# Cross attention and a recurrent block: two attention steps per unit on TensorE, side work reordered

## The reference

```python
q = q.reshape(b, l, KVH, GROUPS, HD).transpose(0, 2, 3, 1, 4)
scores = jnp.einsum('bkgld,bksd->bkgls', q, k) * scale + encoder_attention_mask[:, :, None, :, :]
attn = jax.nn.softmax(scores, axis=-1)
out = jnp.einsum('bkgls,bksd->bkgld', attn, v)
x = _ln(out @ Wo + bo + hidden_state) * gamma + beta            # first layer
xxx = jnp.einsum('blfd,fde->blfe', jnp.tanh((xa + sx * maa_x) @ maa_w1)..., maa_w2)
w = jnp.exp(-jnp.exp(time_decay + jnp.tanh(xw @ td_w1) @ td_w2))
def step(s, rkvw):                                              # 256 tokens in turn
    a = k_t[..., :, None] * v_t[..., None, :]
    out = jnp.einsum('bhi,bhij->bhj', r_t, u * a + s)
    s = a + w_t[..., :, None] * s
    return (s, out)
x1 = x + group_norm(out) * silu(g) @ Wo.T
return x1 + sigmoid(xr2 @ Wfr.T) * (square(relu(xk2 @ Wfk.T)) @ Wfv.T)
```

## Time and profile before

| | us |
|---|---|
| median of the runs | 1290.37 |
| the profiled execution, its own time | 1290.32 |
| its span, first to last instruction | 1288.5 |
| PE busy | 1080.8 (84%) |
| ACT busy | 875.5 (68%) |
| DVE busy | 661.7 (51%) |
| POOL busy | 366.3 (28%) |
| mean granted TensorE clock | 0.933 |

### The profile page before, as it was taken

How to read it: one execution, slowest core, us unless ns; L and a number is a source line. 1 busy time by engine, 2 the same in 40 slices (tenths; PEclk the granted TensorE clock), 3 DMA queues, 4 the chain that set the end, 5 groups by cost and what they waited for, 6 DMA issues and landing times.

```text
span 1288.5 us, 18192 instructions
## 1 busy us (share of the span) xinstructions
PE 1080.8 (84%) x7100; PEld 372.0 (29%) x7100; DVE 661.7 (51%) x1113; ACT 875.5 (68%) x953; POOL 366.3 (28%) x381
## 2 busy tenths in 40 slices
PE   3065999899899989999899989998999989997554
PEld 1011122232233323332233223331433223323312
DVE  5322141647463755556464746476465445454473
ACT  1045989777877777777877787777778877794001
POOL 6103023135111532144203522153213200340270
PEclk9567999999999999999999999999999989998666
DMA  5533405170514323261406141342306020500130
GB/s 186 136 92 114 94 1 141 45 128 2 131 34 101 58 91 66 70 97 46 94 26 131 28 125 40 83 76 92 65 11 97 3 40 11 75 1 1 19 55 10
DMA packets 65565, 87.47 MB, mean 68 GB/s; under 512 B 8208, under 2 KB 48192, under 8 KB 65472
## 3 DMA queue, kind: packets, MB, share of 16 engines
q1 hardware_dynamic: 63536, 82.91, 29.5%
q0 software_dynamic: 1936, 3.32, 0.9%
HBM read 50.74 MB, written 18.62 MB: 54 GB/s over the span
## 4 chain that ended last, share of the span: by engine, by line
PE 58%; ACT 14%; DVE 13%; issue 8%; POOL 3%; DMA 2%; SPq 2%; DVEq 0%; ACTq 0%; POOLq 0%
PE psum L702 56%; ACT probs L640 10%; DVE row_max L1124 3%; PE psum L800 1%; DVE o_raw L1171 1%; PE psum L794 1%; DVE k_c L1220 1%; POOL vs L532 1%; SPq L317 1%; DVE k_stack L1435 1%; DMA ctx_t<-in_mask 1%; ACT L640 1%; POOL vs L544 1%; DMA vs<-v_c 1%; DVE xa L1211 1%
## 5 line engine op out<-in xcount | busy, mean ns | idle before, releaser
L640 ACT ACTIVATE probs<-psum 128x1024 f32<-128x1024 f32 (+1 forms) x832 | 807.1, 1023 | 282.6 <-PE psum L702 279.0
L702 PE MATMUL psum<-probs,v_aug 128*9 128x512 f32 (+1 forms) x3328 | 446.8, 609 | 20.8 <-DVE o_raw L1171 20.6
L702 PE MATMUL psum<-q_stack,k_stack 64*128 64x512 bf16 (+1 forms) x1664 | 323.3, 396 | 49.3 <-ACT probs L640 39.9
L702 PEld LDWEIGHTS psum<-q_stack,k_stack 64*128 64x128 bf16 (+1 forms) x1664 | 83.2, 95 | 520.5 <-ACT probs L640 342.2
L527 POOL TENSOR_TENSOR xm<-tmp,xa 128x512 f32<-128x512 f32 x40 | 42.9, 1091 | 235.8 <-DVE tmp L1231 235.8
L1124 DVE TENSOR_REDUCE row_max<-psum 128x8 f32<-128x1024 f32 x64 | 78.0, 1218 | 53.9 <-PE psum L702 53.6
L544 POOL TENSOR_TENSOR vs<-r_c,vs 128x512 f32<-128x512 f32 x64 | 77.7, 1215 | 91.4 <-DVE vs L1242 91.4
L514 POOL TENSOR_TENSOR rstd<-moments,eps 128x2 f32<-128x2 f32 x24 | 4.9, 206 | 311.5 <-DVE moments L1197 311.5
L1242 DVE TENSOR_TENSOR_SCAN vs<-w_c,vs 128x514 f32<-128x514 f32 x64 | 88.9, 1389 | 3.5 <-POOL vs L532 1.1
L532 POOL TENSOR_TENSOR vs<-k_c,vs 128x512 f32<-128x512 f32 x64 | 83.4, 1308 | 23.6 <-DVE r_c L1373 15.0
L702 PEld LDWEIGHTS psum<-probs,v_aug 128*9 128x9 f32 (+1 forms) x3328 | 50.2, 88 | 126.5 <-issue 106.8
(11 more groups left out here) (175 smaller groups left out, 1134.6 us busy)
## 6 DMA issues: line engine op xcount, KB each, us to landing
vs<-v_c SPq DMA_DIRECT2D x64, 257.0 KB, 7.7
ctx_t<-in_mask SPq DMA_DIRECT2D x8, 1601.0 KB, 7.1
k_stacked<-k_parts SPq DMA_DIRECT2D x48, 200.1 KB
k_stack<-k_stacked SPq DMA_DIRECT2D x32, 300.2 KB, 6.5
ctx_t<-in_ctx_t SPq DMA_DIRECT2D x24, 400.0 KB, 5.0
q_stacked<-q_parts SPq DMA_DIRECT2D x96, 64.0 KB, 2.0
q_stack<-q_stacked SPq DMA_DIRECT2D x32, 192.0 KB, 6.7
ctx_t<-in_ctx_t SPq DMA_DIRECT2D x8, 401.0 KB, 3.3
```

The source lines that it names most:

```text
L640: nc.scalar.activation(probs[turn_step % NP][t][0:w, :, :], ps[t][0:w, :, :], ACT.Exp).then_inc(exped.sem, 1)
L702: return nc.tensor.matmul(dst, lhsT, rhs, start=start, stop=stop)
```

## The change

TensorE now walks the steps in pairs. A unit is: both score tiles of the even step, both weighings of the two steps before, both score tiles of the odd step, one side piece. At two steps where a weighing starts a new group (14 and 40, `DIVIDED`) that weighing stands behind the side piece. Small pieces with few partitions (turning v, sub rounds, the second decay product) are in a new function `score_rows` and stand directly behind score tiles. All side pieces have even steps. ScalarE does its side work after both exps of a step, not between them.

Side work is ordered anew on TensorE, VectorE, ScalarE and SP. Two of the four key/value projections of f stand at step 42, beside the square root on ScalarE. The query projection of f moves from step 0 of the next turn to step 48. The sub rounds of a are at steps 31 to 34 (before 35, 36, 37, 39). The output product moves from step 50 to 46. POOL writes the start state (`first_state`, two copies of four passes each) instead of VectorE, and copies v for the next element after the state passes.

```diff
+DIVIDED = (NC + 1, 3 * NC + 1)
-KV_BANK = 5
-KV_STEP = [34, 36, 38, 40]
-A_ROUNDS = [35, 36, 37, 39]
+KV_BANK = (5, 5, 6, 7)
+KV_STEP = [32, 34, 42, 42]
+A_ROUNDS = [31, 32, 33, 34]
+B_ROUNDS = [12, 13, 14, 15]
@@ gpsimd
+            def first_state(c, j0):
+
+                for j in range(j0, j0 + HD // 2):
+                    pool.wait_ge(spread_in[j].sem, spread_in[j].at(c))
+                nc.gpsimd.tensor_copy(vs[:, j0:j0 + HD // 2, :, 0],
+                                      s_init[:, :, c % B, j0:j0 + HD // 2].rearrange("p e j -> p j e"))
+
             def key_value(c, j):
-                pool.wait_ge(spread_in[j].sem, spread_in[j].at(c))
@@ scalar
                         if b is not None:
                             exp_tile(b, step, 0)
+                            exp_tile(b, step, 1)
                         side(step, c, d)
-                        if b is not None:
-                            exp_tile(b, step, 1)
-                if step == 47:
+                if step == 42:
                     act.wait_ge(o_var.sem, o_var.at(c))
@@ tensor
-                    for step in range(STEPS):
+                    for step in range(0, STEPS, 2):
                         if b is not None:
                             score_tile(b, step, 0, general)
-                        if step >= 2 and b is not None:
+                            score_tile(b, step, 1, general)
+                        score_rows(step - 1, it, lo, general)
+                        if step == 0:
+                            if c is not None:
+                                weigh(c, STEPS - 2)
+                                weigh(c, STEPS - 1)
+                        elif b is not None:
                             weigh(b, step - 2)
-                        elif step < 2 and c is not None:
-                            weigh(c, STEPS - 2 + step)
+                            if step not in DIVIDED:
+                                weigh(b, step - 1)
                         if b is not None:
-                            score_tile(b, step, 1, general)
+                            score_tile(b, step + 1, 0, general)
+                            score_tile(b, step + 1, 1, general)
+                        score_rows(step, it, lo, general)
                         side(step, it, lo, general)
+                        if b is not None and step in DIVIDED:
+                            weigh(b, step - 1)
@@ vector
             def state_pass(c, j):
-                dve.wait_ge(spread_in[j].sem, spread_in[j].at(c))
-                link(nc.vector.tensor_copy(vs[:, j, :, 0], s_init[:, :, c % B, j]))
                 dve.wait_ge(a_ready.sem, a_ready.at(c, j + 1))
...
+                        reduce_step(b, 1, 0, general)
                     if c is not None:
                         dve.wait_ge(xt_turned.sem, xt_turned.at(c))
                         token_differences(c, 1, 5, "ln1_w", "ln1_b")
                     if b is not None:
+                        reduce_step(b, 1, 1, general)
+                        keep_output(b, 0)
+                    if c is not None:
+                        shift_mix(mix, "maa_x", mix_ready)
+                    if b is not None:
+                        reduce_step(b, 1, 2, general)
                         reduce_step(b, 1, 3, general)
                         negate_shift(b, 1)
...
```

More of the change, by code:

```diff
@@ L414, in all_turns @@
                                 load_x_rows(c)
-                        if step == 6 and a is not None:
+                        if step == 8 and a is not None:
                             if it == lo:
@@ L1330, in all_turns @@
                         row_moments(x0, c, 1)
+                    if it > lo and a is not None and not general:
+                        see_mask(a, 0)
                     if it == B and not general:
```

510 lines of the change are left out of this document (272 added, 238 removed).

## The result

The changed kernel takes 1350.4 us (median of 4 runs, 1349.5 to 1352.4) where the kernel before took 1290.6 in runs beside it: a ratio of 1.047 (95% interval 1.045 to 1.0486), 60 us slower. The forecast was 1334, slower by 44, with a range up to 1350: the direction and the main step came out, the size was short by 16 us, and the time lies just above the range. What the forecast had wrong was above all a term that it put at nothing, the normalisation.

The account below looks back on a forecast made before the run. TensorE bounds most stretches, ScalarE nearly as full. Four full turns +14, second +6.3, seventh +1.5, first +8, eighth +8, last stretch +6.5: together +44 on 1288.5, plus 1.8 outside the span, 1334 us; range 1318 to 1350.

Parts of the forecast that it names:

- the main step: Sub round at step 31: TensorE waits 5 to 8 us once per turn for VectorE's bonus, half clock behind it.
- the normalisation: VectorE's operations after the square root: start late, but product asked for only at step 46; no cost.
- The unit's loop: TensorE and ScalarE per two steps: a unit is never shorter than 4.7 us, where the order before needed 3.76.
- The root: ScalarE's square root near step 43: projections cover it, 1.2 us of waiting left, some 4 us per turn gone.
- The stall before step 31: TensorE waits 6.6 us for the bonus, now behind six state passes, with scan and POOL product taking turns.
- Waits for ScalarE in a full turn: Thin units lack 7.5 us, 1.2 is left at the square root, 1.0 for d_sq at step 40.
- The slow clock behind the stall: After TensorE's idle time before step 31 the clock falls: 1.3 us per full turn.
- Steps 13 to 16: TensorE waits for VectorE's reduction and mix at sub round 14 and w1: 2.0 us, bounds 0 and 2.5.
- the four landings: POOL's start-state copy waits for four transfers instead of one: bounds 0 and 3.7 us, taken as 0 in full turns.
- 1.3 for o_raw: The weighing of step 26 waits for o_raw, now behind the first scan: 1.3 us per full turn.
- Seventh +1.5: The seventh turn of attention gets 1.5 us longer.
- The first turn +8: First turn: 19 units at 4.7 against 3.76, mask stall of 11.8 stays, one more mask reduction: 8 us longer.

Follow-up runs that it names:

- the mixed kernel: Changed kernel with VectorE's bonus ahead of pass 4, GpSimd's key split held until og, and 9 thin units alternating: 1283.9 us, ratio 0.9932.
- Split late: Changed kernel with GpSimd's split of the next keys held back until og is finished: 1333.0 us, ratio 1.0321.
- pass by pass: Changed kernel with GpSimd's first states awaited for one or two passes at a time instead of four: 1325.0 us, ratio 1.0274.
- the repairs: Changed kernel with VectorE's bonus ahead of pass 4 and GpSimd's key split held until og, pairs kept: 1294.8 us, ratio 1.0021.
- bonus early: Changed kernel with VectorE's bonus and gate products directly behind the fourth state pass, reductions between later passes: 1310.0 us, ratio 1.0158.
- changed, alternating: Changed kernel with every unit's scores and weighings back to alternating order, side pieces left in place: 1349.0 us, ratio 1.0436.
- the mixed kernel on the side order of before: Kernel before with 19 paired and 7 alternating units per turn, ScalarE's side steps behind both exponentials: 1377.5 us, ratio 1.0662.

## Why the prediction was short

**What held.** The unit's loop: 4.7 forecast, 4.65 measured. Busy time per full turn without slow clock: from 127.0 (129.0 less 2 of slow clock) to 123.3 (127.2 less 2.3 and 1.6), 3.7 less where the unit was to save 3.9. The pair of weighings was 1.84, forecast 1.86. The root is covered (0.96 left, forecast 1.2), and without cover the mixed kernel is 16 us slower. The stall before step 31 was 6.98, forecast 6.6, and released by the instruction named; the passes in front of it ran with scans of 2.2. Waits for ScalarE in a full turn were 8.3, forecast 7.5+1.2+1.0.

**What failed.** The step that failed most is the normalisation, put at nothing: it cost 2.25 us of waiting in each of five turns, 11.2 in all. Three more terms were too small and one turn was not worked out. First, against a full turn of 143.9 that took 147.0:

- *"whose product is asked for only at step 46; not late."* It was late, by 2.25 a full turn. I costed the normalisation with the durations of before and did not ask what GpSimd does beside it once its keys come at step 42. The contention I had priced for the scans holds for these operations as well. Split late takes it away: the lines are back at 0.69 and 0.74, the wait is gone, and 17 us come off, of which some 11 are this wait and the rest, as far as the profiles show, is the clock at w1.
- *The slow clock behind the stall at 1.3.* It was about 2.3 (1.7 on the sixteen weighings alone), since two weighings and two scores fall into it where I had counted one weighing and half a follower.
- *Steps 13 to 16 at 2.0.* The waits were 1.4, but the w1 product ran at the lower clock, 1.6 more: 3.0 in all. I had a price for slow clock and left it out here. It falls in five of the six turns, in two with pass by pass and in none with split late.
- *"bounds 0 and the 3.7 that two more issues take, I take 0"* for the four landings. They held up the first product by 1.9. Pass by pass in the changed kernel takes off 25 us: in a full turn 1.6 of the wait I had put down as 1.3 for o_raw "behind the first scan", 0.5 of the stall, and the slow stretch at w1 in three of the five turns that had it; besides, 3.6 at the end. 3.8 more, in the first turn, are not the edit's. Once the repairs were in, the same edit gave the six turns only 2.6, and with all units alternating nothing. So the zero is right for a pipeline with slack and wrong for this one.
- *Seventh +1.5*, given without a working. It was +7.9 (138.4 to 146.3). It has the whole stall of 7.0 and its slow clock (bonus early brings it to 138.0), and nothing goes at its root, which no projection covers: TensorE waits 3.84 there, and 2.97 in the kernel before.
- *The first turn +8.* It was +11.8 in this profile, and +8.0 to +11.1 in four other kernels with the same order there: the term was about right, and alternating units bring it to 131. The second turn was +7.6 where I had +6.3, the last part +11.1 where I had 14.5; 11.2 of it are one wait for the product of r and k (13.6, before 2.4).

Over the span the forecast was 17.8 short (62.1 against 44.3): 9.7 in the four full turns, 6.4 in the seventh, 3.8 in the first, 1.3 in the second, less 3.4 at the end.

By terms a full turn was 2.25 (og, the output of the normalisation) + 0.4 (stall) + 1.0 (its clock) + 1.0 (steps 13 to 16) + 0.3 (o_raw) too low and 1.2 too high for ScalarE (waits of 8.3 against 9.7, less 0.2 of busy time): 3.75, of which 3.1 was seen.

**Where the 60 us lie.** The unit and the side order do not add up. The unit alone on the kernel before (with ScalarE's order) costs 48 us, the side order alone (changed, alternating) 57, both 60. In the changed kernel the unit costs nothing in sum, for what pairs lose in waits, in the first turn above all, they save in busy time and in waits for og, while the stall keeps its length. With both stalls repaired it costs 11 (1294.8 against 1284.0; 8 by the ratios). Repairing the two stalls of the side order takes off 56 of the 60 us (1350.4 to 1294.8), the slow stretches that go with them included. The pieces are not separate costs: pass by pass alone takes 25 off the same kernel. Repaired, the side order is the better one, 1284.0 with alternating units against 1290.6, and 1274.4 with the first states awaited singly.

**Not settled.** Why the mixed kernel on the side order of before is 39 us slower than the one with pairs everywhere; and what puts the slow stretch at the w1 product in one turn and not in the next. In both, runs show the clock and the short waits in front of it, no more; at w1 the waits are the same whether the stretch is slow or not. Nor was ScalarE's new order (side work behind both exponentials) tried by itself.

The version that beats both is the changed kernel with bonus ahead of pass 4, the split behind og, first states pass by pass, and alternating units: 1274.4 us, ratio 0.99 (0.9858 to 0.9941).

## What to carry to other kernels

When side work moves on one engine, redraw who runs beside whom on VectorE and GpSimd before using any old duration: an operation costed from a quiet place took six times as long in company (0.37 and 2.3 us). A pairing that saves an engine's own time is worth only what the loop with its partner leaves; compare both per unit, thin units first. And price a stall with its slow clock, here a third on top, at every place where it may fall.

## What the runs showed of the hardware

- A tensor_scalar of 128x256 took 0.37 us alone and 2.3 beside GpSimd's work on the keys; a tensor_tensor of 128x512 with both inputs in SBUF 0.69 and 2.16; a scan of 128x514 1.23 and 2.19; a reciprocal of 128x512, 3.34 in both.
- A load of ScalarE's tables took 1.28 us in every kernel; load, root, load 3.3 to the next exponential. Bare of cover, that was 2.9 us more of waiting for TensorE.
- Sixteen weighings in a row take 1.84 us, eight between scores 0.98: 0.12 less for a pair. Behind a wait of 7 us the same sixteen took 3.60, at a granted clock of 0.50 (1.2 GHz); short waits of 0.9 to 2.0 us close together also had it beside them.
